# Multiplying the signs ahead on Pool, casting the last integers on ACT, and moving a small bias product in a vision-transformer tower

## The reference, cut to what matters

```python
def act_qdq(x):
    qmax = 2.0 ** (ACT_BITS - 1) - 1.0
    scale = jnp.maximum(jnp.max(jnp.abs(x)) / qmax, 1e-12)
    return jnp.clip(jnp.round(x / scale), -qmax - 1.0, qmax) * scale
...
x = act_qdq(x)
up = act_qdq(x @ lpbq_dequant(w_up).T)
gate = act_qdq(x @ lpbq_dequant(w_gate).T)
sig = fixed_qdq_u16(jax.nn.sigmoid(gate))
gate = act_qdq(gate * sig)
o = act_qdq(gate * up)
return o @ lpbq_dequant(w_down).T
```

## Time and profile before

| what | value |
|---|---|
| median of three runs | 271.38 us |
| profiled execution, its own time | 273.36 us |
| its span (first to last instruction) | 271.6 us |
| PE busy / its weight loads | 246.0 us (91%) / 201.9 us |
| DVE busy | 197.0 us (73%) |
| ACT busy | 110.3 us (41%) |
| POOL busy | 60.7 us (22%) |

### The profile page before, as it was taken

One profiled execution on the slowest core, in us unless ns is written; L12 is line 12 of the kernel. 1 busy time (PEld: TensorE's weight loads), 2 busy tenths in 40 slices (PEclk: granted clock), 3 DMA queues, 4 the chain that ended last, 5 costly groups with the idle time before them and its releaser, 6 DMA issues.

```text
span 271.6 us, 5576 instructions
## 1 busy us (share of the span) xinstructions
PE 246.0 (91%) x2165; PEld 201.9 (74%) x2165; DVE 197.0 (73%) x481; ACT 110.3 (41%) x266; POOL 60.7 (22%) x119
## 2 busy tenths in 40 slices
PE   4999989899999999999999899989987899956894
PEld 3888769798888687777777688766766777736682
DVE  1876877299435477897897797687776667999881
ACT  2581461235326611111112265827542475979000
POOL 7772521037100030000000015496400000610000
PEclk9999977955799999999999999999999999995999
DMA  6949850000000910000000000000000000000002
GB/s 174 276 103 290 253 193 2 2 2 0 2 5 1 311 39 0 0 0 0 2 0 0 1 2 0 4 2 0 2 2 4 0 0 0 0 0 4 1 2 87
DMA packets 14429, 12.02 MB, mean 44 GB/s; under 512 B 2952, under 2 KB 13859, under 8 KB 14403
## 3 DMA queue, kind: packets, MB, share of 16 engines
q1 hardware_dynamic: 14333, 11.62, 14.7%
q10 hardware_dynamic: 70, 0.05, 0.1%
HBM read 11.05 MB, written 0.61 MB: 43 GB/s over the span
## 4 chain that ended last, share of the span: by engine, by line
PE 72%; DVE 16%; issue 4%; ACT 4%; POOL 2%; DVEq 0%; POOLq 0%; ACTq 0%
PE bank L1887 48%; PE bank L1973 5%; PE bank L2057 4%; PE bank L1882 4%; PE bank L2429 3%; PE bank L2121 2%; PE bank L2104 2%; DVE big L1843 1%; DVE big L1838 1%; DVE big L1777 1%; POOL big L658 1%; DVE keys_n L1768 1%; ACT big L1101 1%; PE bank L2090 1%; PE bank L2032 1%
## 5 line engine op out<-in xcount | busy, mean ns | idle before, releaser
L1887 PE MATMUL bank<-xT,big 128*128 128x296 f32 (+1 forms) x192 | 46.4, 392 | 0.4 <-DVE keys_n L1594 0.4
L1887 PEld LDWEIGHTS bank<-xT,big 128*128 128x128 f32 x192 | 34.1, 190 | 10.3 <-issue 0.7
L696 POOL TENSOR_SCALAR big<-keys_n,k_w 128x256 f32<-128x256 f32 x24 | 16.6, 711 | 63.3 <-DVE keys_n L1594 63.3
L926 ACT ACTIVATE cen<-bank 128x296 f32<-128x296 f32 x20 | 8.4, 418 | 45.1 <-PE bank L1887 41.2
L1887 PE MATMUL bank<-xT,fT 128*128 128x296 f32 (+12 forms) x96 | 24.6, 416 | 0.5 <-DVE xT L1739 0.5
L1887 PE MATMUL bank<-big,cur 128*128 128x256 f32 (+1 forms) x100 | 23.2, 380 | 1.0 <-DVE cur L1481 1.0
L1887 PEld LDWEIGHTS bank<-xT,fT 128*128 128x128 f32 x96 | 17.2, 191 | 7.0 <-issue 1.8
L1887 PEld LDWEIGHTS bank<-big,cur 128*128 128x128 f32 (+1 forms) x100 | 18.1, 182 | 5.0 <-DVE cur L1481 1.5
L1882 PE MATMUL bank<-ident,ones 128*128 128x128 f32 x88 | 15.7, 344 | 5.8 <-POOL rsd L587 4.0
L1882 PEld LDWEIGHTS bank<-ident,ones 128*128 128x128 f32 x88 | 14.6, 253 | 6.2 <-POOL rsd L587 4.0
L1494 DVE SCALAR_TENSOR_TENSOR h<-bank,route,h 128x256 f32<-128x256 f32 (+1 forms) x40 | 17.0, 478 | 3.0 <-PE bank L1887 3.0
(11 more groups left out here) (334 smaller groups left out, 516.7 us busy)
## 6 DMA issues: line engine op xcount, KB each, us to landing
big<-in_x SPq DMA_DIRECT2D x3, 576.0 KB, 7.9
big<-in_L_ffn_w_gate SPq DMA_DIRECT2D x2, 512.0 KB, 7.0
big<-in_L_ffn_w_up SPq DMA_DIRECT2D x2, 512.0 KB, 7.1
big<-in_L_ffn_w_down SPq DMA_DIRECT2D x1, 1024.0 KB, 5.5
small<-in_L_tok_lin_w SPq DMA_DIRECT2D x3, 256.0 KB, 5.3
small<-in_L_ffn_w_gate SPq DMA_DIRECT2D x1, 768.0 KB, 4.6
small<-in_L_ffn_w_up SPq DMA_DIRECT2D x1, 768.0 KB, 6.4
small<-in_L_ffn_w_down SPq DMA_DIRECT2D x1, 768.0 KB, 7.7
```

Source lines behind the costliest of these rows:

```text
L696: ins = pool.tensor_scalar(fkeys[a - 1][:, u, :, n, :], keys, k_w[:, a - 1, n:n + 1], 1.0, ALU.mult, ALU.mult)
L926: empty(act.activation(silu[:, c, :], b[:, 0:HP], ACT.Silu))
L1887: ins = pe.matmul(out_, a_, b_, start=(n == 0), stop=(n == len(pairs) - 1))
```

## The change

There are four edits:

- **The small biases move** behind the turn of half 1, on PE, on DVE and in `fills()`.
- **POOL makes all four parts of `gate_mag`.** DVE's instruction for part 0 goes. On ACT the sigmoid of part 0 now stands ahead of the copy of up bank 0, and the sign of that bank behind all four sigmoids.
- **POOL multiplies the signs ahead**: `sign_gate *= sign_up`, bf16, columns 0 to 2559 as soon as the signs of up banks 0 to 4 are there and POOL has done its half part of `silu_mag`, columns 2560 to 3551 when the last sign is there.
- **The eight last pieces** need one DVE instruction each (scale, sign, round to int32), and ACT casts them to floats.

The diff, without the new semaphores and the helper `o_piece` that names a piece:

```diff
@@ fills()
-        if u == 0:
+        if u == 1:
             f.append((("bl",), "dve"))
@@ POOL
-            for n, (lo, hi) in enumerate(PARTS[1:], 1):
-                pool.wait_ge(gate_on_grid, 1 if n == 1 else 3)
+            for n, (lo, hi) in enumerate(PARTS):
+                pool.wait_ge(gate_on_grid, 1 if n < 2 else 3)
                 pool.tensor_scalar(gate_mag[:, lo:hi], gate_abs[:, lo:hi], qs[:, 1, 1:2], 1.0,
                                    ALU.mult, ALU.mult).then_inc(magnitudes_on_grid_pool, 1)
...
+            for n, (lo, hi) in enumerate(((0, UC[4][1]), (UC[4][1], FN))):
+                if n == 0:
+                    pool.wait_ge(up_signed, 4)
+                else:
+                    emptied(pool, ("up", len(UC) - 1))
+                pool.tensor_tensor(sign_gate[:, lo:hi], sign_gate[:, lo:hi], sign_up[:, lo:hi],
+                                   ALU.mult).then_inc(signs_multiplied, 1)
@@ ACT
-            b = take(act, ("up", 0))
-            act.activation(up[:, 0:512], b[:, :], ACT.Abs).then_inc(first_up_copied, 1)
-            empty(act.activation(sign_up[:, 0:512], b[:, :], ACT.Sign))
-
             for n, (lo, hi) in enumerate(PARTS):
...
+                if n == 0:
+                    act.activation(up[:, 0:512], take(act, ("up", 0))[:, :], ACT.Abs).then_inc(first_up_copied, 1)
+
+            empty(act.activation(sign_up[:, 0:512], bank_of(("up", 0))[:, :], ACT.Sign))
...
+            for n, at_ in enumerate(o_pieces):
+                act.wait_ge(o_on_grid, n + 1)
+                v = o_piece(gate, at_)
+                act.copy(v, v.bitcast(I32)).then_inc(o_ready, 1)
@@ DVE
-            small_biases()
             for t in range(1, RT, 2):
                 probs_turned(1, t)
+            small_biases()
...
             for n in range(len(PARTS)):
-                if n == 0:
-                    of_magnitudes = mark(scaled(part_of(gate_mag, n), part_of(gate_abs, n), 1))
                 up_maximum(n)
-                if n == 0:
-                    after(of_magnitudes)
-                else:
-                    dve.wait_ge(magnitudes_on_grid_pool, n)
+                dve.wait_ge(magnitudes_on_grid_pool, n + 1)
...
-            emptied(dve, ("up", len(UC) - 1))
-            for at_ in pieces:
-                link(signed_by_gate(at_))
-                signed_by_up(at_).then_inc(o_ready, 1)
+            for n, at_ in enumerate(o_pieces):
+                dve.wait_ge(signs_multiplied, 1 if n < 2 else 2)
+                v = o_piece(gate, at_)
+                dve.scalar_tensor_tensor(out=v.bitcast(I32), in0=v, scalar=qs[:, 4, 1:2], in1=o_piece(sign_gate, at_),
+                                         op0=ALU.mult, op1=ALU.mult).then_inc(o_on_grid, 1)
```

More of the change, by code:

```diff
@@ L482, in build @@
         o_ready = sem("o_ready")
+        o_on_grid = sem("o_on_grid")
+        up_signed = sem("up_signed")
+        signs_multiplied = sem("signs_multiplied")
         df_ready = sem("df_ready")
@@ L502, in take, with o_piece @@
             return bank_of(key)
+        o_pieces = [(o, o + 2, 0) for o in range(0, FC, 2)] + [(o, o + 3, 1) for o in (0, 3)] + [(0, FC, t) for t in range(2, TT)]
+        def o_piece(buf, at_):
+            lo, hi, t = at_
+            return buf.rearrange("p (o t) -> p o t", o=FC)[:, lo:hi, t * P:min((t + 1) * P, NT)]
         def patch_columns(k, g):
@@ L1096, in _ @@
             for c in range(1, len(UC) - 2):
-                up_signs(c)
+                up_signs(c).then_inc(up_signed, 1)
             act.wait_ge(silu_scaled, 1)
```

## The result

Four runs of the changed kernel gave 274.58 to 274.96 us, median 274.67; four of the kernel before in the same comparison 268.84 to 272.15, median 271.52. The ratio is 1.0146, with an interval of 1.008 to 1.0212: the change made the kernel 3.15 us slower. The forecast was 275.0 us. The profiled execution of the changed kernel took 274.62 us.

The account below looks back on a forecast made before the run. PE was taken as the bound (72% of the span), waiting on DVE, ACT or POOL in the last stage. Terms -0.3 - 0.5 + 4.7 + 0.3 - 0.6 = +3.6 us on the median 271.4 gave 275.0 us, range 270.9 to 277.1.

Parts of the forecast that it names:

- small biases: First attention: bias products move from half clock to full clock, so the values of half 0 start earlier; -0.3 us.
- magnitudes: Last stage: POOL makes all gate magnitudes and the sigmoid goes first, so the first product starts earlier; -0.5 us.
- first multiplication: Last stage: POOL's 2560-column sign product takes 5.2 us and holds DVE's 480-column scaling until it ends; +4.7 us.
- second multiplication: Last stage: POOL's 992-column sign product, behind DVE's last product, makes the first last piece wait; +0.3 us.
- last pieces: Down product: one DVE instruction a piece, so no piece is late and PE has no gap; -0.6 us.
- its other case: Magnitudes: POOL runs its parts without letting DVE in, DVE's last gate scalings start 1 us later; costs 0.4 us.
- A cheap multiplication: Rival: the first sign product runs at the one-source price, 3.2 us, holding DVE 2.7; 272.7 us, chance 0.17.
- No hold: Rival: POOL's multiplication lets DVE's 480-column scaling through, so the kernel is faster; -1.4 us, 270.0 us, chance 0.14.
- An earlier clock: Rival: in the first attention the clock rises before the values of half 0; up to 1.7 less, 273.3 us, chance 0.10.
- POOL ahead of the last product: Rival: POOL's second multiplication gets in before DVE's last product; +2.0 us more, 277.0 us, chance 0.09.

Follow-up runs that it names:

- the later comparison: The changed kernel once more, unaltered, beside the kernel before on the same chip: median 276.41 us against 273.13, ratio 1.0207.
- the version with 256 columns: The changed kernel with POOL's first sign product of 2560 columns cut into ten parts of 256: median 278.15 us, ratio 1.0179.
- the run with the later product: The changed kernel with POOL's uncut 2560-column sign product moved behind the scale of up: 279.34 us in one run.

## Why the prediction was right, step by step

The forecast was 3.6 us slower and 275.0 us; it became 3.15 slower and 274.67. That the absolute time was met to 0.3 us is in part luck: in the later comparison the same kernel took 276.41, outside the forecast's own range of 274.2 to 275.6. By the traces the forecast was 0.6 too high, nearly all of it in the first multiplication. The steps of its sum, each taken from the same two events in both traces:

| step | forecast | measured | how |
|---|---|---|---|
| small biases | -0.3 | -0.26 | start of the first turns to start of the values of half 1: 11.70, 11.44 |
| magnitudes | -0.5 | -0.35 | start of the up columns to the first maximum spread: 13.06, 12.71 |
| first multiplication | +4.7 | +4.11 | from there to ACT's magnitudes: 4.09, 8.20 |
| second multiplication | +0.3 | +0.25 | from there to the first last piece: 6.70, 6.95 |
| last pieces | -0.6 | -0.79 | from there to the end of the down product: 14.98, 14.19 |
| sum | +3.6 | +2.96 | |

- **Small biases.** As worked out: one wait is exchanged for less work at full clock. The turns start at 62.33 and 60.56; the values of half 1 at 74.03 and 72.00. Over all traces this length is 11.36 to 11.65 with the edit, and 11.70 and 11.82 in the two without it.
- **Magnitudes.** The step that was mis-sized is "product 0 starts at 234.84, 1.06 earlier". It starts 6.40 us after the up columns instead of 6.84, only 0.44 earlier, since POOL's second part got in ahead of DVE's last scaling of gate, which took 1.32 us for 480 columns. This is half of what the prediction had as its other case ("if POOL runs its parts without letting DVE in"), priced there at +0.4. The part that made up for it was "each get in between products and cost about 0.5 together": the later POOL parts held the products by 0.1 us in all. The run with POOL's magnitudes later took away just this wait, and the first product then started 0.87 us earlier (5.54 us after the up columns, 6.41 without it).
- **First multiplication.** The mechanism was right, and the run of half its size shows it best: 2.42 us off the product, 2.41 off the stage. "5.2 us" for the product was 5.02, 0.18 less. "DVE stands from 244.2 to 248.9", that is to POOL's end with its own work still to come; in the trace the held instruction ended 0.27 behind POOL's end, not the 0.46 to 0.55 that this implies, 0.2 less. And "Nothing hides it" left out a cover of 0.2: DVE's next instruction waits for PE's spread, and before it started at 245.24, 0.10 after the scaling's end; now it starts at 247.00, as the scaling ends. From one start to the other it was 0.56 us, and is 4.68: 4.12 more, which is the 4.11 of the table.
- **Second multiplication.** POOL's part started at 252.52, 0.25 behind DVE's last product (252.27), as the forecast's margin of 0.2 had it. Its cost fell on DVE's last step of the scale, which was held until POOL's end at 254.84: 0.40 us instead of 0.16, 0.24 of the 0.25. The first piece itself was not held.
- **Last pieces.** No gap, as forecast. The down product takes 13.22 us, 0.2203 each: I had 0.2225 each from the 36 behind the gap in the earlier trace rows, which had waits of their own.

**The profiled execution above the median.** I set the difference on the median, not on the profiled time that lay 2.0 us higher. The traces bear that out. From the first turns on, the two traces differ by 3.0 us; ahead of the turns, where nothing was edited, the changed kernel was 62.33 - 60.56 = 1.77 us faster, so the two profiled times differ by 1.26 only (273.36 and 274.62). Windows from 34 to 50, before and then after:

```profile
34.00:50.00 16.00, 14.70 (x294) 13.03 (x295) 10.06 (x33) 6.35 (x21) 2.95 (x5) 0.79 0.26 83
```
```profile
34.00:50.00 16.00, 13.30 (x302) 12.24 (x301) 10.20 (x30) 6.41 (x21) 2.37 (x4) 0.89 0.22 72
```

The granted clock was 0.79 in the one and 0.89 in the other, a different share of time at half clock in each execution. Over the twelve traces the turns start anywhere from 60.3 to 63.0. In the two traces of the changed kernel they start 1.33 us apart (60.56 and 61.89) and the executions took times 1.30 apart (274.62 and 275.92), so there this is the whole difference, and it lies ahead of every edit. What makes these stretches differ is not shown.

**The rivals.** A cheap multiplication: it took 1.96 ns a column, at the two-source price of the earlier trace rows. No hold: it fell with 4.76 us for 0.46. The rule of the Trainium skill ("SBUF - State Buffer", section "Who interferes with whom"), that the hold lasts for the whole instruction, agrees with the trace at 2.60 and at 5.02 us. The estimate from its "GPSIMD Engine Reference" (section 3.1), 5.6 us, was 12% too high. An earlier clock: the values of half 0 took 4.17 us in place of 4.00. POOL ahead of the last product: it came 0.25 behind.

The middle of the kernel, from the values of half 1 to the up columns, took 155.03 us before and 155.04 after.

## What to carry to other kernels

Before work is moved to POOL, look at what DVE does beside it. In this kernel a POOL instruction held until its end DVE's scaling of 480 columns, its products of two tensors, its copy of 128 x 2 and its `tensor_tensor` of one element, while reductions, one-element scalings and reciprocals passed. If a held instruction is on the chain, the price is the POOL instruction's length less what DVE needed or waited for anyway. Cutting it into small instructions turns one long hold into many small ones; that helped here by 1 of 3.2 us, and the eleven parts took POOL 12.1 us in place of 7.3. And whenever the chain changes its length, see whether the unread products that keep PE busy still reach to its end.

## What the runs showed that I had not expected

- **The size of the DVE instruction does not matter.** A `tensor_tensor` of one element per partition stood for 4.99 us beside POOL's product of 2560 columns, where it takes 0.15 alone. Its kind does: beside POOL's second product one-element instructions of three other kinds were not held. In each scale's chain only its last step is a `tensor_tensor`.
- **bf16 is not faster on POOL.** The product costs 5.02/2560 = 1.96 ns a column and 2.60/1280 = 2.03, the fp32 products of the earlier trace rows 2.02 to 2.10.
- **POOL gets in between two DVE instructions that stand back to back**, and DVE between two of POOL's: in the changed kernel the scaling at 231.37 had to wait behind POOL's second part, and in the version with 256 columns DVE passed between POOL's parts all the way.
- **DVE holds POOL as well.** POOL's second product started 0.25 behind DVE's last product and took 2.32 us. Less the 0.40 until that product ended (252.92), it is 1.92 us, or 1.94 ns a column, near the 1.96 of the first.
- **A gap of 2.2 us on PE cost 2.7 us later, where the clock was still low.** Behind it the down product ran its first 5.6 us at a granted clock of 0.50. With twelve more unread products the clock was at 1.00 before they ended, a gap of 2.10 us followed, and the down product ran at 1.00 throughout. A gap of 6.21 us in the run with the later product was followed by a loss of 1.24 only, so the length of the gap alone does not set the price.
